# First stages of a graph network kernel: three waits taken apart, and the split of the edge attributes put on GpSimd

## The reference

```python
# block 0: attention with edge features
h = (x @ W.T).reshape(n, H, D)                         # "table0" of the kernel, with score columns
alpha = einsum(h[src], a_src) + einsum(h[dst], a_dst)
enc = relu(edge_attr @ edge_W.T + edge_b)              # the edge attributes that the kernel splits
alpha = alpha + sum(enc * h[dst], axis=-1)
alpha = where(alpha >= 0, alpha, 0.2 * alpha)
attn = segment_softmax(alpha, dst)
out = segment_sum(h[src] * attn, dst) + bias
x = layernorm(x + out)
# blocks 1 and 2: sums over neighbours, done with an adjacency matrix
agg = segment_sum(x[src], dst); deg = segment_sum(1, dst)
h = (agg / max(deg, 1)) @ Wl.T + bl + x @ Wr.T
```

## Time and profile before

| | us |
|---|---|
| median of 3 runs | 3785.88 (3781.16 to 3790.82) |
| the profiled execution | 3784.86 |
| its span | 3782.9 |
| VectorE's set-up, start to end | 31.85 to 55.4 |
| table tiles, first and last copy by ScalarE | 15.89 to 92.0 |
| adjacency, first matmul to last copy | 92.04 to 296.2 |
| first matmul of node rows in the edge stage | 316.49 |

### The profile page before, as it was taken

The page is one execution under the profiler, slowest core; times in us unless marked ns, Lnnn a source line. Parts: engine busy times, 40 slices in busy tenths (PEclk is TensorE's granted clock), DMA queues, the critical chain, the costliest instruction groups (busy, mean ns, idle before and its releaser), DMA issues.

```text
span 3782.9 us, 60200 instructions
## 1 busy us (share of the span) xinstructions
PE 3144.3 (83%) x16284; PEld 1885.8 (50%) x16285; DVE 2042.5 (54%) x5112; ACT 1151.9 (30%) x2974; POOL 1586.2 (42%) x1461
## 2 busy tenths in 40 slices
PE   3876989888879999999999999658888756778866
PEld 3333555555544445445445445445555434555543
DVE  3996888888852110111115211446666655666666
ACT  1543454444411001001001100254444335444433
POOL 0993565555413004004001200167777536777730
PEclk7997999999969999999998999768787867888876
DMA  5325776666502321321330232245454324555521
GB/s 176 128 115 179 197 195 194 192 193 191 163 1 86 103 84 62 101 87 55 103 95 10 77 102 77 67 110 143 137 141 138 101 68 121 140 140 138 139 65 35
DMA packets 226151, 439.48 MB, mean 116 GB/s; under 512 B 61018, under 2 KB 137359, under 8 KB 225725
## 3 DMA queue, kind: packets, MB, share of 16 engines
q1 hardware_dynamic: 165309, 263.16, 22.4%
q0 software_dynamic: 60544, 173.03, 17.0%
HBM read 391.96 MB, written 44.08 MB: 115 GB/s over the span
## 4 chain that ended last, share of the span: by engine, by line
PE 47%; DVE 14%; POOL 12%; issue 11%; SPq 9%; DMA 4%; ACT 2%; DVEq 1%; POOLq 0%; ACTq 0%
PE ps L705 25%; POOL rows L1996 12%; PE ps L778 3%; PE ps L939 3%; DVE norm L1389 3%; SPq L1867 3%; PE ps L556 2%; PE ps L591 2%; PE ps L919 2%; SPq L1868 2%; PE ps L889 2%; DMA rows<-table,src_idx 2%; PE ps L881 2%; DVE inv L1646 1%; DVE spread L1379 1%
## 5 line engine op out<-in xcount | busy, mean ns | idle before, releaser
L1996 POOL DMA_INDIRECT rows<-table,src_idx x1248 | 1383.7, 1109 | 710.3 <-issue 361.9
L705 PE MATMUL ps<-rows,rT 128*128 128x504 f16 (+1 forms) x3200 | 884.7, 363 | 16.4 <-DMA rows<-adjacency 16.4
L705 PE MATMUL ps<-rows,spread 128*128 128x504 f16 (+1 forms) x1600 | 580.0, 362 | 0.0
L705 PEld LDWEIGHTS ps<-rows,rT 128*128 128x128 bf16 x3200 | 312.6, 98 | 341.7 <-issue 22.6
L1409 DVE TENSOR_TENSOR rows<-ps,norm 128x72 f32<-128x72 f32 x312 | 71.9, 233 | 663.7 <-PE ps L705 661.8
L1953 POOL CAST rT<-rows 128x1024 bf16<-128x1024 f32 (+1 forms) x28 | 26.6, 950 | 939.9 <-ACT rows L1165 939.9
L778 PE MATMUL ps<-rows,spread 128*128 128x260 f32 x832 | 304.7, 516 | 28.6 <-DVE rows L1540 28.1
L556 PE MATMUL ps<-rT,spread 128*128 128x272 f32 x832 | 254.3, 431 | 42.8 <-DMA rT<-table 22.0
L778 PE MATMUL ps<-rows,w_roots 128*128 128x260 f32 x832 | 265.0, 461 | 21.0 <-DVE rows L1540 19.1
L1540 DVE TENSOR_TENSOR rows<-rows,ps 128x1024 f32<-128x1024 f32 x208 | 251.4, 1209 | 17.8 <-ACT rows L1067 16.6
L591 PE MATMUL ps<-rows,rT 128*128 128x272 f32 x832 | 244.9, 443 | 2.3 <-DVE rows L1263 2.3
(11 more groups left out here) (252 smaller groups left out, 4767.8 us busy)
## 6 DMA issues: line engine op xcount, KB each, us to landing
rows<-adjacency SPq DMA_DIRECT2D x140, 630.0 KB, 3.8
rT<-table SPq DMA_DIRECT2D x416, 136.0 KB
spread<-in_tiles SPq DMA_DIRECT2D x104, 256.0 KB, 3.6
rows<-table,src_idx POOLq DMA_INDIRECT x1248
w_table<-in_tiles SPq DMA_DIRECT2D x52, 256.0 KB
adjacency<-rT SPq DMA_DIRECT2D x4, 3150.0 KB, 9.8
adjacency<-acc SPq DMA_DIRECT2D x4, 3150.0 KB, 11.1
table<-rows SPq DMA_DIRECT2D x12, 528.0 KB, 3.0
```

The lines of the kernel that those rows point to most:

```text
L705: ins = mm(chunk_ps[c % 2][:, f, 0:width], xp[k][:, t, f * P:(f + 1) * P], ring[q][:, i, 0:width], start=t == 0 and k == 0, stop=t == ROWS ...
L1996: pool.indirect_dma_start(src_rows(l, par)[:, k, :], None, tables[l][:, :], bass.IndirectOffsetOnAxis(ap=src_idx[:, g * T + k:g * T + k + ...
```

## The change

Four things are edited.

1. `store_tables(sp, -1)` moves on SyncE from behind the set-aside stores and `w_enc` to right behind the loads. The four stores of VectorE's tables count on a new semaphore `tables_aside`, the twelve of the split parts on `aside`. ScalarE's adjacency copies wait for `tables_aside` first, and for `aside` at the first pack of the stage that lies in acc.
2. The eight index loads count on `indices_loaded`, the other twelve on `loaded`. VectorE's set-up waits for the first alone; its four small copies of score columns, which need `loaded`, move behind `tables_ready`.
3. GpSimd makes the split of the edge attributes, before its gathers, and raises `attr_split`; SyncE waits for that before it stores the parts.
4. The waits for both adjacency stores are taken apart. ScalarE and SyncE's spans wait for the store of the stage in rT alone, VectorE only for ScalarE's copies. acc is cleared by GpSimd, behind the first four groups' gathers and a wait for the last store; VectorE's first rescaling waits for it (`acc_cleared`).

The diff, without the new semaphores' declarations and the eight loads that only change their helper:

```diff
 FROM_ACT_STAGES = [3, 4, 5, 6]
-LOADS = 20
+INDEX_LOADS = 8
+LOADS = 12
 LOADED = 16 * LOADS
...
 HEAD = D // 8 + 1
-ASIDE = 16 * (4 + 3 * 4)
+TABLES_ASIDE = 16 * 4
+ASIDE = 16 * 3 * 4
 SUM_BUFS = 4
...
+ADJ_STORED = 16 * NCK // 2
...
             pe.wait_ge(row_out, ROWS * (l + 1))
+            pe.wait_ge(tables_aside, TABLES_ASIDE)
             pe.wait_ge(aside, ASIDE + 16)
...
                         act.wait_ge(consts, CONSTS)
+                        act.wait_ge(tables_aside, TABLES_ASIDE)
                         act.wait_ge(aside, ASIDE)
...
         def adjacency_act(act):
-            act.wait_ge(aside, ASIDE)
+            act.wait_ge(tables_aside, TABLES_ASIDE)
             for j in range(PACKS):
                 c, i = divmod(j, CP)
+                if i == 0 and c == 1:
+                    act.wait_ge(aside, ASIDE)
                 if i == 0 and c > 1:
...
                 node = V.value_load(base[0:1, bass.ds(g, 1)], min_val=0, max_val=N)
+                if isinstance(g, int) and g == 0:
+                    dve.wait_ge(acc_cleared, 1)
                 dve.wait_ge(resc_copied, g + 1)
...
+            def load_index(dst, src):
+                sp.dma_start(dst, src).then_inc(indices_loaded, 16)
+
             for n, s in enumerate((0, 5, 6)):
...
                 sp.dma_start(xT[:, :, lo:lo + n], a["xT"][:, lo:lo + n].rearrange("(f p) n -> p f n", p=P)).then_inc(x_loaded[i], 16)
...
             load(bias[:, :, :], a["biases"].rearrange("p (l f) -> p l f", f=FC))
...
             assert n_loads[0] * 16 == LOADED, n_loads
+            store_tables(sp, -1)
             sp.wait_ge(tables_ready, 1)
-            sp.dma_start(in_tiles[:, :], in_tile).then_inc(aside, 16)
-            sp.dma_start(pen_rows.rearrange("(p j) w -> p j w", j=4), pens_of_tile).then_inc(aside, 16)
+            sp.dma_start(in_tiles[:, :], in_tile).then_inc(tables_aside, 16)
+            sp.dma_start(pen_rows.rearrange("(p j) w -> p j w", j=4), pens_of_tile).then_inc(tables_aside, 16)
             for j in range(2):
-                sp.dma_start(pen_ends[j:j + 1, :].rearrange("o (p k) -> (o p) k", k=4), ends_of_tile[:, j, :]).then_inc(aside, 16)
+                sp.dma_start(pen_ends[j:j + 1, :].rearrange("o (p k) -> (o p) k", k=4), ends_of_tile[:, j, :]).then_inc(tables_aside, 16)
+            sp.wait_ge(attr_split, 1)
             for k in range(PARTS):
...
                 sp.dma_start(w_edge_parts[k], w_edge_part[:, k, :]).then_inc(aside, 16)
+            sp.wait_ge(tables_aside, TABLES_ASIDE)
             sp.wait_ge(aside, ASIDE)
...
                     sp.dma_start(to, made).then_inc(adj_stored[c % 2], 16)
-                for b in range(2):
-                    sp.wait_ge(adj_stored[b], 16 * NCK // 2)
...
                 sp.dma_start(attr[:, par, :], attr_parts[:, bass.ds(x * T * P, T * P)]).then_inc(attr_landed[par], 16)
+                if early and x == 0:
+                    sp.wait_ge(adj_stored[0], ADJ_STORED)
                 for q in range(4):
...
                 if l == 0:
-                    store_tables(sp, -1)
                     store_adjacency()
...
                     inverses_out()
+                    sp.wait_ge(adj_stored[1], ADJ_STORED)
                     for m in SUMS:
...
             pool.sem_inc(seg_free, 2)
+            pool.wait_ge(indices_loaded, 16 * INDEX_LOADS)
             pool.wait_ge(loaded, LOADED)
             splitting = Steps(pool, split_step)
+            for rest, part_of in ((attr_rest, attr_part), (w_edge_rest, w_edge_part)):
+                for k in range(PARTS):
+                    splitting.then(nc.gpsimd.tensor_copy(part_of[:, k, :], rest))
+                    if k < PARTS - 1:
+                        splitting.then(nc.gpsimd.tensor_tensor(rest, rest, part_of[:, k, :], ALU.subtract))
+            pool.sem_inc(attr_split, 1)
...
                         wait_alone(pool, near_turned, 4 * (l - 4))
+                    if l == 0 and g == SUM_BUFS:
+                        wait_alone(pool, adj_stored[1], ADJ_STORED)
+                        nc.gpsimd.memset(acc[:, :, :], 0.0).then_inc(acc_cleared, 1)
                     if g >= SUM_BUFS:
...
             act.wait_ge(loaded, LOADED)
-            for b in range(2):
-                act.wait_ge(adj_stored[b], 16 * NCK // 2)
+            act.wait_ge(adj_stored[0], ADJ_STORED)
             for l in range(n_edge_layers):
...
             ins.then_inc(built, 1)
-            dve.wait_ge(loaded, LOADED)
-            dve.wait_ge(built_pe, 2)
-            for n in (1, 2):
-                for m in range(FC):
-                    ins = V.tensor_copy(w_table[4 + n][:, m, D:D + 8], ps[:, 1 + n, 8 * m:8 * m + 8])
-            ins.then_inc(built, 1)
+            dve.wait_ge(indices_loaded, 16 * INDEX_LOADS)
             V.tensor_scalar(floor[:, :], deg_row[:, 0:1], 1e-10, None, ALU.max)
...
             V.tensor_scalar(tile_base[:, :], dst_idx[0:1, :], NPAD - P, None, ALU.min)
-            for rest, part_of in ((attr_rest, attr_part), (w_edge_rest, w_edge_part)):
-                for k in range(PARTS):
-                    ch.then(V.tensor_copy(part_of[:, k, :], rest))
-                    if k < PARTS - 1:
-                        ch.then(V.tensor_tensor(rest, rest, part_of[:, k, :], ALU.subtract))
             for at, x, y in ((0, slice(1, P + 2), slice(0, P + 1)), (P + 1, slice(1, P + 1), slice(0, 1)),
...
             dve.sem_inc(tables_ready, 1)
-
+            dve.wait_ge(loaded, LOADED)
+            dve.wait_ge(built_pe, 2)
+            for n in (1, 2):
+                for m in range(FC):
+                    ins = V.tensor_copy(w_table[4 + n][:, m, D:D + 8], ps[:, 1 + n, 8 * m:8 * m + 8])
+            ins.then_inc(built, 1)
             turns, sum_turns, more_turns = Turns(dve, "dve_turns"), Turns(dve, "dve_sum_turns"), Turns(dve, "dve_more_turns")
...
             adjacency_dve(dve)
-            dve.wait_ge(aside, ASIDE)
-            for b in range(2):
-                dve.wait_ge(adj_stored[b], 16 * NCK // 2)
-            V.memset(acc[:, :, :], 0.0)
+            dve.wait_ge(adj_copied, 2 * PACKS)
             for l in range(n_edge_layers):
...
                 if LAYERS[l][0] == "gat_edge":
```

More of the change, by code:

```diff
@@ L295, in gnn_program @@
         aside = sem("aside")
+        tables_aside = sem("tables_aside")
+        indices_loaded = sem("indices_loaded")
+        acc_cleared = sem("acc_cleared")
+        attr_split = sem("attr_split")
         turned_hot_ready = sem("turned_hot_ready")
@@ L1782, in _ @@
                 sp.dma_start(xT[:, :, lo:lo + n], a["xT"][:, lo:lo + n].rearrange("(f p) n -> p f n", p=P)).then_inc(x_loaded[i], 16)
-            load(src_idx[:, :], a["src_idx"])
-            load(dst_idx[:, :], a["dst_idx"])
-            load(base[:, :], a["base_row"].partition_broadcast(P))
-            load(last[:, :], a["last_row"])
-            load(pack[:, :], a["pack_row"].partition_broadcast(P))
-            load(last_of_pack[:, :], a["last_pack_row"].partition_broadcast(P))
-            load(dst_by_group, a["dst_groups"])
-            load(seg_of_tile, a["dst_seg"].rearrange("(p j) w -> p j w", j=4))
+            load_index(src_idx[:, :], a["src_idx"])
+            load_index(dst_idx[:, :], a["dst_idx"])
+            load_index(base[:, :], a["base_row"].partition_broadcast(P))
+            load_index(last[:, :], a["last_row"])
+            load_index(pack[:, :], a["pack_row"].partition_broadcast(P))
+            load_index(last_of_pack[:, :], a["last_pack_row"].partition_broadcast(P))
+            load_index(dst_by_group, a["dst_groups"])
+            load_index(seg_of_tile, a["dst_seg"].rearrange("(p j) w -> p j w", j=4))
             load(bias[:, :, :], a["biases"].rearrange("p (l f) -> p l f", f=FC))
```

## The result

The changed kernel takes 3745.8 us (median of 4 runs, 3743.18 to 3746.67) against 3784.74 of the kernel before beside it: 38.9 us less, ratio 0.990 (95% interval 0.9888 to 0.9913). The profiled execution took 3743.18, with a span of 3741.4. Forecast were 3739, in 3725 to 3753: the sign and the place are right, and 46.5 us were promised where 38.9 came (33 to 42 by the interval). The time lies 0.8 us above the forecast's own 3732 to 3745. The profile says where most of the other 7.6 went. In the kernel after, the lines have new numbers: L1176 is the copy of table tiles, L947 their matmul, L693, L1392, L1402 and L1115 are matmul, lo_hot, key and copy of the adjacency, L1838 its store, L1212 the one-hot, L564 the spread of node rows, L2025 the gathers.

A forecast was written before the change was run, and what follows sets the result against it. Bound: a front where ScalarE idled 50.46 us for the first table store, then VectorE's adjacency stage. 41.2 - 0.6 + 5.9 = 46.5 off 3784.86 gives 3738.4, with the median's offset 3739; own range 3732 to 3745, full range 3725 to 3753.

The forecast's parts named there:

- Part 1: Front: table stores go ahead of SyncE's wait, the first lands at 32.3, adjacency starts at 50.8, 41.2 us earlier.
- rival A: Load and store queue: transfers don't queue, first table store lands at 26.2, small ones pass the big store; 3728; chance 0.15.
- rival C: Adjacency stage: TensorE still at the 1.2 GHz level and the bound, 114 us slower, 3853; chance 0.03.
- Part 2: VectorE's set-up: index loads land near 20.5, ready at 43.0, eight microseconds of cover before 50.8; costed at nothing.
- Part 3: Adjacency start: ScalarE's copies wait for tables_aside, landing at 57.0; 0.6 us charged, bounds 0 to 3.
- Part 4: Split on GpSimd: 15 us from 31.9, done at 47 undisturbed, attr_split needed by 63; costs nothing undisturbed.
- rival B: Split beside VectorE's keys: GpSimd is starved, or holds VectorE up; middle 3749; chance 0.15.
- rival B's second case: VectorE waits for GpSimd's split instead: 5 us lost, 3744; chance 0.15 for the whole rival.
- Part 5: Edge stage start: waits for the last adjacency store taken apart, first L556 at 310.6 instead of 316.49, 5.9 us earlier.
- signs of being wrong: Adjacency stage grows by over 3 us, or stages behind the edge stage's start don't keep their length.

The follow-up runs named there:

- e6: The changed kernel with the eight index loads moved ahead of xT's chunks 2 to 6; 3739.6 us.
- e3: The changed kernel with one more wait: GpSimd clears acc only when VectorE has made the first group's one-hots; 3745.13 us.
- e7: e6 with the four tables_aside stores issued between the table stores of chunks 2 and 3 instead of behind the last; 3740.72 us.
- e9: The edits of e6 and e8 together on the changed kernel; 3738.37 us, ratio 0.9876 to the kernel before.
- e4: The changed kernel with the waits for the last adjacency store put back and VectorE clearing acc again; 3751.93 us.
- e1: The changed kernel without the split: ScalarE makes six casts in its place and the subtractions are left out; 3743.02 us.
- e2: The changed kernel with the split back on VectorE in its old place, behind a wait for the loads; 3743.34 us.
- e8: The changed kernel with the last adjacency store issued behind the first group's eleven edge-stage loads instead of ahead; 3737.08 us.

## Why the prediction was right, and where its sum was off

- *Part 1, right, the last step by luck.* The store was issued at 25.59 and landed at 33.4 (32.3 predicted); the clock was back 3 us after the restart, not 5, which made up for it: two misses cancelled, and the tables ended at 50.83, where 50.8 was the start forecast. The store landed 7.8 us behind its issue instead of 1.86, so the transfers queued and rival A is out, and rival C with it: TensorE was at full clock 14 us ahead of the first key.
- *Part 2, the step that failed.* "I cost it at nothing" rested on eight microseconds of cover. The index loads landed at 24.5, not 20.5: bytes issued over the rate of the window gave a landing 4 us too early, and I had no row of a landing there. Four microseconds went there and 9.7 to GpSimd, against a cover of 8: 5.7 lost at the keys, 5.0 seen at the last store once part 3's 0.6 is taken off. With VectorE ready in time only 2.5 of them came back (e6), as ScalarE's wait for tables_aside stood right behind.
- *Part 3.* First copy at 59.55 instead of 57.0, because pen_ends was issued and landed later (the row names PE; the same row of e3, at 59.60, names pen_ends). Hidden in the changed kernel, where VectorE was late anyway. As soon as VectorE is not, it is worth 1.6 us where TensorE's clock held (e6 against e7) and 3.5 where it fell (e9 against e7), and not the 0.6 charged.
- *Part 4, right on GpSimd, wrong on VectorE.* GpSimd's last cast ended at 53.14, ahead of 63, with no gap at ScalarE's 15th pack. What I had as rival B's second case, VectorE waiting, is what the trace shows: 5 us lost, and its 3744 is nearer to 3745.8 than my 3739. The row that I had (gathers of 7.71 against 0.95) shows GpSimd waiting beside keys; I took it as the likely direction for casts and subtractions, and it doesn't say that. The Trainium skill, "SBUF — State Buffer", section "Who interferes with whom", has it that the one that issues first holds the shared ports for its whole instruction. The trace agrees that each waits in full for the other, in both directions, with the 3.21 us of a 0.18 us copy and the 1.88 us on GpSimd's subtraction. That the first to issue wins it doesn't show: by the rows the subtraction starts at 35.38, ahead of L2145 at 35.52, and is the one that waits.
- *Part 5, right mechanism, gain 3.6 instead of 5.9.* high_row landed at 273.3 (12.15 behind its issue), attr near 274.6, 13.9 behind the store's issue, and 14.0 was forecast for all; from the store's issue to L564 16.6, not 14.3. Of the missing 2.3 up to 2.1 are GpSimd's memset (L564's wait of 2.09 for the one-hot): it starts as the store lands, 2.3 us ahead of the one-hot, and lasts 5.64. No run shows L564 without it and with the gathers done. I had asked who waits for its result, and covered that by 36 us, and not whom it disturbs while it runs. It took 5.64 us (6.2 forecast), and nobody waited for acc_cleared: the rescaling ran at 317.40 with 0.25 us of idle before it.
- *The sum.* 46.5 less 5.0 less 2.3 is 39.2, which is the shift at L564 (39.17). The median's 38.9 is near, but its interval is 33 to 42.
- *The range.* The time came out 0.8 us above the forecast's own 3745, and in the range because that took in the middle of rival B. One of the prediction's signs of being wrong came true: from the first key matmul to the last store it is 208.4 us and not 204.2, over the 3 us of growth that it allowed. The 4.2 us lie at the start of the stage, where TensorE had no keys in hand; before it had eight.

## What to carry to other kernels

An operation that moves to an engine off the path isn't free if the two engines hold each other up, as VectorE and GpSimd did here (0.18 us became 3.21): price both engines for the time in which they overlap, for the moved operation (part 4) and for a clearing that nobody waits for (part 5). A cover of a few microseconds is an estimate minus an estimate; count a landing from a row, and ask what bound stands next behind the one removed, as here three (VectorE, tables_aside, the tables) lay within 5 us. And of a large transfer ask what stands behind it in the queue: issued after the small loads instead of before, the store gave 9 us at the next stage's start, of which no run shows how much is left at the end.

## What the runs showed of the hardware

- VectorE and GpSimd held each other up in whole instructions: 0.15 to 0.23 us became 1.5 to 3.4 beside casts and subtractions, a one-hot 0.75 became 3.6 to 5.7 beside a memset, and seven keys 2.63 became 12.11 beside the split (e6). VectorE's three comparisons of 104x516 and 104x512 (L2145, 1.88 us) were not held: there GpSimd waited.
- Beside gathers it is the other way round: the keys keep their 2.63 us for seven, and a gather of 0.95 takes 7.71.
- Gathers on GpSimd beside keys on VectorE get through unevenly. Many take 7.71 us, one a period, but single ones took 51.39, 83.47 (e4), 115.53 (e1) and 131.56 us (e3) in kernels whose key stage is alike, and 0 to 21 of 32 were left at its end. What decides it stays open. Where the edge stage's first load stands right behind the big store, it landed 11.4 to 12.2 us after its issue with none left (changed kernel, e2, e6), and 13.4 to 14.7 with 7 to 21 left (e1, e3, e7).
- A 256 KB load behind the 3150 KB store took 12.15 us to land, and 3.8 ahead of it (e8), with nine gathers running then.
